# Loading the first block of x once and writing its shifted planes on chip, in a fused five-stage kernel

## What is computed

```python
h = tok(x)                      # patches of 16 steps at stride 8 -> 32 tokens of 256; two dense layers
h = h + attn(layernorm(h))      # ternary weights, activations rounded to 8 bits, 16 heads
h = h + ffn(layernorm(h))       # top-1 of 8 experts, 100 places each, one shared expert matrix
h = h + ssm(layernorm(h))       # a decaying complex scan over the 32 tokens
h = h + moe(layernorm(h))       # top-2 of 8 experts, SwiGLU
```

## Time and profile before

| | |
|---|---|
| median of 3 runs | 497.02 us (496.32 to 497.54) |
| the profiled execution, its own time | 495.51 us |
| its span, first to last instruction | 493.8 us |
| PE busy | 426.9 us (86%) |
| DVE busy | 287.7 us (58%) |
| ACT busy | 200.7 us (41%) |
| POOL busy | 170.5 us (35%) |
| chain that ended last, its largest engine | PE 53% |
| the chain's share of loading x | 4.0% |

### The profile page before, as it was taken

The page is one execution under the profiler, slowest core; times in us unless marked ns, Lnnn a source line. Parts: engine busy times, 40 slices in busy tenths (PEclk is TensorE's granted clock), DMA queues, the critical chain, the costliest instruction groups (busy, mean ns, idle before and its releaser), DMA issues.

```text
span 493.8 us, 9446 instructions
## 1 busy us (share of the span) xinstructions
PE 426.9 (86%) x3489; PEld 264.0 (53%) x3490; DVE 287.7 (58%) x885; ACT 200.7 (41%) x373; POOL 170.5 (35%) x141
## 2 busy tenths in 40 slices
PE   0879999798777874788889999999999999999991
PEld 0535556456464663645546766666654544456650
DVE  0498777587688999999996488527751111111110
ACT  1224744464467533335534653255323232333330
POOL 6042010010010116742154536443254565556331
PEclk9999999999996966798999999999999999999997
DMA  9999410029028100463011422162132222322211
GB/s 166 256 203 201 81 48 3 1 59 327 7 65 320 29 23 1 149 233 132 8 47 41 109 35 51 24 136 45 20 56 33 44 37 44 47 44 43 43 23 21
DMA packets 35468, 40.22 MB, mean 81 GB/s; under 512 B 5216, under 2 KB 30048, under 8 KB 35296
## 3 DMA queue, kind: packets, MB, share of 16 engines
q1 hardware_dynamic: 26192, 29.91, 22.8%
q0 software_dynamic: 7040, 9.44, 12.0%
q10 hardware_dynamic: 2192, 0.27, 0.6%
HBM read 28.47 MB, written 8.91 MB: 76 GB/s over the span
## 4 chain that ended last, share of the span: by engine, by line
PE 53%; DVE 18%; DMA 13%; issue 6%; ACT 5%; SPq 3%; POOLq 0%; POOL 0%; DVEq 0%; ACTq 0%
PE psum L2347 19%; PE psum L2368 10%; PE psum L1942 9%; DMA out_dram<-O,dst_i 5%; DMA M3s<-in_x_dram 4%; DMA out_dram<-O,dst_high 3%; PE psum L1956 3%; PE psum L2357 2%; PE psum L1968 2%; PE psum L1986 2%; DVE st_att L1054 1%; PE psum L2329 1%; SPq L334 1%; DVE H L1297 1%; DVE Eb L1094 1%
## 5 line engine op out<-in xcount | busy, mean ns | idle before, releaser
L1835 DVE TENSOR_TENSOR QT<-QT,psum 128x512 f32<-128x512 f32 x36 | 24.7, 687 | 116.6 <-PE psum L2347 114.2
L2368 PE MATMUL psum<-M3s,KT 128*128 (+1 forms) x352 | 69.3, 383 | 1.4 <-ACT KT L846 0.8
L2347 PE MATMUL psum<-M1s,KT 128*128 (+2 forms) x176 | 68.9, 601 | 1.8 <-issue 1.5
L2347 PE MATMUL psum<-M2s,KT 128*128 (+2 forms) x176 | 67.7, 592 | 0.0
L2368 PEld LDWEIGHTS psum<-M3s,KT 128*128 128x128 f32 (+1 forms) x352 | 50.2, 170 | 24.5 <-issue 16.8
L1942 PE MATMUL psum<-M2s,M1s 128*128 128x512 f32 x128 | 58.7, 602 | 1.0 <-ACT H L714 0.7
L857 ACT ACTIVATE O<-psum,gate_slot 128x256 f32<-128x256 f32 x36 | 17.1, 475 | 100.4 <-PE psum L2368 91.8
L516 POOL DMA_INDIRECT KT<-mixture_rows_in,src_i x36 | 40.5, 1125 | 32.2 <-issue 18.3
L2347 PEld LDWEIGHTS psum<-M2s,KT 128*128 128x128 f32 (+1 forms) x176 | 26.0, 171 | 35.8 <-issue 35.8
L543 POOL DMA_INDIRECT out_dram<-O,src_i x17 | 31.5, 1855 | 33.9 <-ACT O L857 14.3
L842 ACT ACTIVATE QT<-psum 128x512 f32<-128x512 f32 x36 | 21.5, 597 | 40.2 <-PE psum L2347 40.2
(11 more groups left out here) (438 smaller groups left out, 764.6 us busy)
## 6 DMA issues: line engine op xcount, KB each, us to landing
M3s<-in_x_dram SPq DMA_DIRECT2D x4, 1024.0 KB, 13.2
M3s<-in_L_ffn_W_dram SPq DMA_DIRECT2D x1, 4096.0 KB, 15.8
M2s<-in_L_ffn_W_dram SPq DMA_DIRECT2D x1, 4096.0 KB, 15.2
M1s<-in_L_ffn_W_dram SPq DMA_DIRECT2D x1, 4096.0 KB, 14.4
M3s<-in_x_dram SPq DMA_DIRECT2D x4, 992.0 KB, 16.5
M1s<-vtok SPq DMA_DIRECT2D x64, 34.0 KB, 1.9
out_dram<-H SPq DMA_DIRECT2D x4, 512.0 KB, 4.2
M1s<-in_L_tok_W_dram SPq DMA_DIRECT2D x2, 512.0 KB, 14.5
```

The source lines that it names most:

```text
L1835: v.tensor_tensor(sil[:, u, :], sil[:, u, :], bank[3], ALU.mult).then_inc(v_gated, 1)
L2347: last = mm(z[rows, :], xrT[:, u, c, rows], w[:, e, c, :].rearrange("p a h -> p (a h)"), start=(c == 0), stop=(c == CH - 1))
L2368: last = mm(bank[6][rows, 0:DM], actT[:, u, c, rows], M3s[:, e, c, :].rearrange("p a d -> p (a d)"), start=(c == 0), stop=(c == HC - 1))
```

## The change

The first block of x is loaded once, to the lower partitions. `sort_first` on both engines writes each plane of block 0 in two copies of 64 partitions: one from the block to the lower partitions, one, shifted by eight steps, to the upper ones, with a separate copy for the last token. The other loads keep their order. The scaling of the ternary weights goes from DVE to ACT. ACT's slot 0 becomes `hidden(0)`, the scaling, `hidden(1)`, `pad(1)`, `embed(0)`, `sort_x(1)`, and then the exponential of the decay. DVE makes the scan vector of the exponential and the mean of the weights ahead of the biases, mixes the bias split with the scan vectors, and sorts block 1 right behind the ternary weights. PE's warm-up waits for the constants in place of x and has 96 columns; the sum of the absolute weights comes two planes into the second output half.

```diff
--- before.py
+++ after.py
@@ -291,8 +291,8 @@
         a_slot_out, a_embed, a_expert, a_k_masked, a_part = (
             sem(n) for n in "a_slot_out a_embed a_expert a_k_masked a_part".split())
 
-        a_sorted, v_biases, a_plane, v_plane = (
-            sem(n) for n in "a_sorted v_biases a_plane v_plane".split())
+        a_sorted, v_biases, a_plane, v_plane, v_weight_scale, a_weights = (
+            sem(n) for n in "a_sorted v_biases a_plane v_plane v_weight_scale a_weights".split())
 
         block = ctx.enter_context(nc.Block())
 
@@ -335,7 +335,7 @@
                 sp.dma_start(xin[64:128, i % 2, :, 0:T_IN - STRIDE],
                              xv[:, SB * i:SB * (i + 1), STRIDE:T_IN]).then_inc(s_x, 16)
 
-            load_x(0)
+            sp.dma_start(xin[0:64, 0], xv[:, 0:SB, :]).then_inc(d_x0, 16)
             for s in range(2):
                 sp.dma_start(W1s[64 * s:64 * s + 64], w1_v[s]).then_inc(d_w1, 16)
             for n, w in enumerate((w_q, w_k, w_v, w_o)):
@@ -579,18 +579,25 @@
             a = nc.scalar
             def pad(i):
 
-                act.wait_ge((d_x0, d_x1)[i % 2], 32 * (i // 2 + 1))
+                act.wait_ge((d_x0, d_x1)[i % 2], 32 * ((i + 1) // 2) + (16 if i % 2 == 0 else 0))
                 a.activation(xin[64:128, i % 2, :, T_IN - STRIDE:T_IN],
                              xin[64:128, i % 2, :, T_IN - STRIDE - 1:T_IN - STRIDE].to_broadcast([64, SB, STRIDE]),
                              ACT.Copy).then_inc(a_pad, 1)
 
+            def sort_first():
+
+                act.wait_ge(d_x0, 16)
+                a.activation(xr[64:128, 0, :, :, L - 1],
+                             xin[0:64, 0, :, T_IN - 1:T_IN].rearrange("p b (r t) -> p r b t", r=1)
+                             .to_broadcast([64, STRIDE, SB, 1]).rearrange("p r b t -> p r (b t)"),
+                             ACT.Copy).then_inc(a_pad, 1)
+                for r in range(RH):
+                    a.activation(xr[0:64, 0, r], xin_r[0:64, 0, r], ACT.Copy)
+                    a.activation(xr[64:128, 0, r, :, 0:L - 1], xin_r[0:64, 0, r, :, 1:L], ACT.Copy).then_inc(a_plane, 1)
+
             def sort_x(i):
 
                 act.wait_ge(a_pad, i + 1)
-                if i == 0:
-                    for r in range(RH):
-                        a.activation(xr[:, 0, r], xin_r[:, 0, r], ACT.Copy).then_inc(a_plane, 1)
-                    return
                 wait(act, p_layer1, CH * (i - 1))
                 a.activation(xr[:, i % 2, 0:RH], xin_r[:, i % 2, 0:RH], ACT.Copy).then_inc(a_sorted, 1)
 
@@ -601,11 +608,7 @@
             act.dma_start(b1c[:], b1.rearrange("(c p) -> p c", p=P), allow_slow_non_contiguous=True).then_inc(d_b, 16)
             act.dma_start(biases[:, 0, :], b2.partition_broadcast(P)).then_inc(d_b, 16)
             act.dma_start(biases[:, 1, :], b_expert.partition_broadcast(P)).then_inc(d_b, 16)
-            pad(0)
-            sort_x(0)
-            act.wait_ge(v_exp, 1)
-            a.activation(sv[:, 4, :], sv[:, 5, :], ACT.Exp, scale=-1.0).then_inc(a_decay, 1)
-
+            sort_first()
             act.wait_ge(d_b, 48)
 
             def exps(i, batches):
@@ -670,19 +673,36 @@
                 iA, iB, iC, iD, iN, iS = (step_of(slot, lag) for lag in LAGS)
                 together = iB is not None and iD is not None
 
+                def embed(i):
+                    for k in range(2):
+                        act.wait_ge(p_layer2, TS * i + 2 * (k + 1))
+                        r = a.activation(H[:, TS * i + 2 * k:TS * i + 2 * k + 2, :].rearrange("p t d -> p (t d)"),
+                                         bank[6 + k], ACT.Copy)
+                    r.then_inc(a_embed, 1)
+
                 def hidden(c):
                     act.wait_ge(p_layer1, CH * iA + c + 1)
                     wait(act, p_layer2, TS * iA)
                     a.activation(h1T[:, c, :], bank[6 + c], ACT.Relu, bias=b1c[:, c:c + 1]).then_inc(a_hidden, 1)
 
-                if iA is not None:
+                if iA == 0:
+                    hidden(0)
+                    act.wait_ge(v_weight_scale, 1)
+                    for w in range(4):
+                        r = a.activation(wraw[:, w, :], wraw[:, w, :], ACT.Copy, bias=MAGIC, scale=wmi[:, w:w + 1])
+                    r.then_inc(a_weights, 1)
+                    hidden(1)
+                    pad(1)
+                    embed(0)
+                    sort_x(1)
+                    act.wait_ge(v_exp, 1)
+                    a.activation(sv[:, 4, :], sv[:, 5, :], ACT.Exp, scale=-1.0).then_inc(a_decay, 1)
+                elif iA is not None:
                     if iA + 1 < STEPS:
                         pad(iA + 1)
                     if iC is not None and not together:
                         exps(iC, range(0, 2))
                     hidden(0)
-                    if iA == 0:
-                        hidden(1)
                     if iA + 1 < STEPS:
                         sort_x(iA + 1)
                 if iN is not None and not (iN <= 1):
@@ -708,15 +728,7 @@
                         r = a.activation(x1[:, t, :], x1[:, t, :], ACT.Copy, bias=MAGIC, scale=SB1["s"][:, t:t + 1])
                     r.then_inc(a_in_quant, 1)
 
-                def embed(i):
-                    for k in range(2):
-                        act.wait_ge(p_layer2, TS * i + 2 * (k + 1))
-                        r = a.activation(H[:, TS * i + 2 * k:TS * i + 2 * k + 2, :].rearrange("p t d -> p (t d)"),
-                                         bank[6 + k], ACT.Copy)
-                    r.then_inc(a_embed, 1)
-
                 if iA == 0:
-                    embed(0)
                     for c in range(CH):
                         act.wait_ge(p_ternaryT, c + 1)
                         a.activation(WT[:, c].rearrange("p w d -> p (w d)"), bank[4 + c].bitcast(BF16), ACT.Copy
@@ -921,6 +933,13 @@
                 dve.wait_ge(g_pow, asked[0] - later)
 
 
+            def sort_first():
+
+                dve.wait_ge(d_x0, 16)
+                for r in range(RH, STRIDE):
+                    v.tensor_copy(xr[0:64, 0, r], xin_r[0:64, 0, r])
+                    v.tensor_copy(xr[64:128, 0, r, :, 0:L - 1], xin_r[0:64, 0, r, :, 1:L]).then_inc(v_plane, 1)
+
             def sort_x(i):
 
                 dve.wait_ge(a_pad, i + 1)
@@ -936,20 +955,6 @@
 
             dve.wait_ge(d_att, 64)
             v.tensor_reduce(wsum[:], wraw, AX, ALU.add, apply_absolute_value=True).then_inc(v_abs_sum, 1)
-
-            dve.wait_ge(d_b, 48)
-            hi, mid = bias_part[:, 0], bias_part[:, 1]
-            ln(v.tensor_copy(hi, biases))
-            own()
-            ln(v.tensor_tensor(bias_rest, biases, hi, ALU.subtract))
-            own()
-            ln(v.tensor_copy(mid, bias_rest))
-            ln(v.tensor_scalar(bias3[:], hi, ident[:, 0:1], None, ALU.mult))
-            own()
-            ln(v.tensor_tensor(bias_rest, bias_rest, mid, ALU.subtract))
-            ln(v.scalar_tensor_tensor(bias3[:], mid, ident[:, 1:2], bias3[:], ALU.mult, ALU.add))
-            own()
-            v.scalar_tensor_tensor(bias3[:], bias_rest, ident[:, 2:3], bias3[:], ALU.mult, ALU.add).then_inc(v_biases, 1)
 
             dve.wait_ge(d_vec, 96)
             pr, pim = vec[:, 0, :], vec[:, 1, :]
@@ -960,15 +965,30 @@
             ln(v.tensor_scalar(t[8], pim, -1.0, None, ALU.mult))
             own()
             v.tensor_tensor(t[5], t[5], t[6], ALU.add).then_inc(v_exp, 1)
+
+            dve.wait_ge(p_abs_sum, 1)
+            own(ln(v.tensor_scalar(wm[:], bank[2][:, 0:4], 1.0 / (DM * DM), 1e-5, ALU.mult, ALU.max)))
+            v.reciprocal(wmi[:], wm[:]).then_inc(v_weight_scale, 1)
+
+            dve.wait_ge(d_b, 48)
+            hi, mid = bias_part[:, 0], bias_part[:, 1]
+            ln(v.tensor_copy(hi, biases))
             ln(v.tensor_tensor(t[7], t[7], pr, ALU.max))
             ln(v.tensor_tensor(t[8], t[8], pim, ALU.max))
             own()
+            ln(v.tensor_tensor(bias_rest, biases, hi, ALU.subtract))
             ln(v.tensor_tensor(t[9], t[7], t[8], ALU.max))
             own()
+            ln(v.tensor_copy(mid, bias_rest))
+            ln(v.tensor_scalar(bias3[:], hi, ident[:, 0:1], None, ALU.mult))
             ln(v.tensor_scalar(t[10], t[9], 0.0, None, ALU.is_equal))
             own()
+            ln(v.tensor_tensor(bias_rest, bias_rest, mid, ALU.subtract))
+            ln(v.scalar_tensor_tensor(bias3[:], mid, ident[:, 1:2], bias3[:], ALU.mult, ALU.add))
             ln(v.tensor_tensor(t[9], t[9], t[10], ALU.add))
             own()
+            v.scalar_tensor_tensor(bias3[:], bias_rest, ident[:, 2:3], bias3[:], ALU.mult, ALU.add).then_inc(v_biases, 1)
+
             ln(v.reciprocal(t[11], t[9]))
             own()
             ln(v.tensor_tensor(t[12], pr, t[11], ALU.mult))
@@ -981,18 +1001,12 @@
             own()
             ask(v.tensor_tensor(t[2], t[14], t[15], ALU.add))
 
-            dve.wait_ge(p_abs_sum, 1)
```

(21 more changed lines are left out.)

## The result

The changed kernel took 498.96 us in the median of 22 runs (497.11 to 501.02), the kernel before 497.28 us (495.62 to 498.40) beside it. The ratio is 1.0037, with a 95% interval of 1.0025 to 1.0049. The forecast was 495.5 us with a range up to 498.0; it was wrong in its sign and in its range. The profiled execution took 498.59 us with a span of 496.8, 3.0 more than before.

A forecast was written before the change was run, and what follows sets the result against it. The start was taken as bound by W1's arrival and by x block 1's pad ahead of ACT's relu. 5.0 (load) - 2.0 (RT block) - 1.5 (clock) = 1.5 us gained: 497.02 to 495.5 us, range 493.4 to 498.0.

The forecast's parts named there:

- One load fewer: At the start, dropping the upper half of x block 0 brings W1 and all behind it 5.0 us earlier.
- Planes, warm-up, bias, ternary weights: Start of the kernel: extra plane copies, later warm-up and reordered DVE work stay hidden and cost PE nothing.
- Relu ahead of the pad: Layer 2 begins at t+15.0 instead of t+16.8 (t: first layer 1 matmul); DVE allows some 0.6 us of gain.
- The wait that takes their place: Late exponential holds POOL's RT block, hence rstd_in and PE's first batch mean: loss 2.0 us, ends 1.4 and 5.5.
- the pair of tensor_scalars: POOL's two RT operations, 4.97 us before, take 1.5 in all with DVE idle; ends 0.9 and 4.97.
- The clock: PE idles 3.8 us ahead of the first batch mean, its clock falls to half speed: loss 1.5 us.
- Sum at the first query matmul: Total of the start's terms: 5.0 from the load, less 2.0 for the RT block and 1.5 for clock, gains 1.5 us.
- D: POOL's tensor_scalars keep 4.97 us, clock falls: 499.0 to 500.2 us; the change gains only below 3.0 for the pair; chance 0.10.
- C: PE starts layer 1 at half clock after the gap ahead of W1: 1.5 us more, 497.0 us; chance 0.14.
- E: At the start, the saved load is not worth 5.0; W1 comes only 2.5 us earlier: 498.0 us; chance 0.06.
- B: POOL's RT block is no bound, a_decay comes before DVE asks: gain 5.0 + 0.6, 491.4 us; chance 0.08.
- A2: PE's clock stays at full speed, idle ahead of the batch mean being nearer 2.5 us: 494.0 us; chance 0.22.

The follow-up runs named there:

- e5: e1 with the upper half of x block 0 loaded again, unread, and 170 instead of 52 warm-up matmuls; 496.06 us, 0.9995 of the kernel before.
- e1: Changed kernel with ACT's decay exponential moved early, right behind the first relu; 491.89 us, 0.9897 of the kernel before.
- e2: Changed kernel with the exponential left late but POOL's RT block moved behind the two roots of step 0; 492.86 us, 0.9918 of the kernel before.
- e8: e1 with pad(1) put back ahead of the second relu; 493.12 us, 0.9933 of the kernel before.
- e10: Kernel before the change with only its decay exponential moved late, behind embed of step 0; 499.95 us, 1.0077 of the kernel before.
- e7: Changed kernel with the second of POOL's two RT tensor_scalars cut to one column; 498.76 us, 1.0056 of the kernel before.
- e11: Changed kernel measured again without any edit, in a later group of runs; 499.66 us, 1.0051 of the kernel before.
- e14: Changed kernel with 92 instead of 52 warm-up matmuls; 500.24 us, 1.0055 of the kernel before.
- e6: e1 with POOL's RT block moved in front of the first power on POOL's list; 491.47 us, 0.9914 of the kernel before.

## Why the prediction was wrong, step by step

**One load fewer.** Mis-sized: W1 came 3.84 earlier, not 5.0 (e5 against e1: 4.2). I took the transfers to stand strictly one behind another. In the changed kernel the lower half lands at 10.08 and not 8.9, with the same start. Between 2 us and the landing of W1 the DMA engines moved 2.64 MB (the windows view: 12.96 us at 204 GB/s) for 2.10 MB of x and W1; before it was 3.47 MB (16.8 us at 207) for 3.11. So 0.5 MB of other transfers had gone along, 0.2 MB more than before, which at 0.2 MB a microsecond is about the missing one. This is worked out and not tried.

**Planes, warm-up, bias, ternary weights.** Right: none shows as a releaser of PE. The copies across partitions cost what copies within them do, 0.61 on DVE and 1.12 on ACT, for half the partitions. DVE's first began at 10.08 and the last ended at 16.35; PE wanted it at 18.5. ACT began only at 10.89, since its own DMA issues took until 9.56 and a table load stood behind them; that was unforeseen and hidden. DVE was through earlier than forecast: its request for the root came at t+21.7, forecast "t+24.1 at the latest", so the 0.6 us that the prediction allowed the relu's move was too little (e2: 1.8).

**Relu ahead of the pad.** Right, at t+15.0 as worked out, and e8 gives its price on the end: 1.2 us, once POOL's block is out of the way. In the changed kernel it bought idle time only.

**The wait that takes their place.** The mechanism is right to a tenth: a_decay at t+22.9 (forecast t+23.0), PE at the batch mean at t+23.5 (t+23.4). The term that failed is the pair of tensor_scalars, 3.05 us against 1.5. I had scaled from other operations, a memset and an affine_select. Half of the row itself, 2.5, which the prediction called an upper reading, was the nearest and still too short; 1.5 missed by 1.55 and the full 4.97 by 1.92. e10 gives 3.04 as well. By the Trainium skill (GPSIMD Engine Reference, 3.1 "Elementwise") 0.43 us each was my estimate; the measurement, 1.53 each with DVE idle, differs by a factor of 3.5 and decides. The batch mean came at t+28.5 in place of t+27.2.

**The clock.** Right that it fell, and mis-sized: 1.9 us here and 1.7 to 2.5 in e7, e10, e11 and e14, against 1.5. The forecast took the 2.9 us that the warm-up had been slow; the windows view shows 4.1 us of work at a granted clock of 0.50.

**Sum at the first query matmul.** Forecast -5.0 + 2.0 + 1.5 = -1.5. Measured -3.84 + 3.3 + 2.2 = +1.66, where 3.3 is t+28.54 less t+25.23, and 2.2 the 1.9 of the 14 matmuls with 0.3 of the batch mean's own. Each of the three terms missed in the same direction, by 1.2, 1.3 and 0.7. The chances had treated them one by one: the range let a single one fail.

**The rivals.** D forecast 499.0 to 500.2 from a pair that keeps 4.97. It came to 3.05, on D's own point of decision of 3.0, where D has no gain and no loss; the loss is the shortfall of the load and the longer slow stretch. That the measured time stands beside D's is luck. C, layer 1 at half clock, happened in three of the ten traces of changed kernels with 52 warm-ups and one load, and cost 1.7 there. Of E's shortfall of 2.5 us in the load, 1.2 came. B is excluded by e1, A2 by PEclk.

**One row misled.** The 2.6 us of idle time at 33.0 that kept the clock was read as a bound; e10 lost it behind 1.95, e11 behind 2.15, while e8 kept it behind 2.94.

## What to carry to other kernels

When an instruction is moved later on its engine, follow its semaphore to the waiting engine and read what stands behind that wait in its list: here 0.20 us on ACT held a block on GpSimd, and that block held the one root that TensorE needed. Price such a block from its own row and not from other operations: even half of that row was too low here. Add up the errors that lie on one chain in one direction. A gap opened on TensorE cost its length and, where the clock fell, 1.7 to 2.5 us more, behind a gap of 1.95 us as behind one of 4.99. So a gain of a few microseconds that ends in a gap can end as a loss.

## What the hardware did that I had not expected

POOL and DVE slow each other on both sides: beside DVE's sort the memset took 1.61 instead of 0.95 and the pair 4.40 instead of 3.05, while the sort took 4.17 instead of 2.77 (e1 against the changed kernel; in e6, beside the bias chain, the pair took 3.35). e10 shows the same for the kernel before: with the RT block moved away from them, the four scalings on DVE took 1.68 instead of 2.89, the two cuts 1.23 each instead of 1.49 and 1.58, and the sort 2.79 instead of 3.04. The Trainium skill (GPSIMD Engine Reference, 8 "Key points") says that POOL shares its SBUF interfaces with DVE and that they contend when DVE is in a two-port mode or has two SBUF inputs; the traces agree that the two engines slow each other, with DVE's sort paying 1.4 us. In which mode the sort ran no trace shows.

Idle stretches of nearly the same length at the same place kept the clock in one execution and lost it in another (ahead of W1: 1.92 and 1.99 kept, 1.98 and 2.15 lost), and at another place 2.94 kept it (e8). The length alone doesn't decide. Nor does the clock fall only while PE is idle. In e7 (start and length of the stretch, PE's busy time with instructions, granted clock, DMA share, GB/s) it was at full speed through the idle stretch of 3.78 us and the first 1.3 us of work, and fell then:

```profile
38.30:42.10 3.80, 0.04 (x1) 1.00 1.12 210
42.10:43.40 1.30, 1.28 (x5) 1.00 1.14 189
43.60:46.80 3.20, 3.20 (x5) 0.50 1.13 207
```

e10 went the same way: 1.00 from 46.2 to 47.6, behind its idle stretch, and 0.50 from 47.8 to 51.0. So it is not enough to look at the clock in the idle stretch itself.
